# First layer norms of batches 4 to 7 one iteration later, keys of batch 1 ahead of the fourth row-max step

## What is computed

```python
x = x + _L0_xattn_ref(_layernorm(x), ctx_1024, ctx_1024, ...)   # 16 heads of 16, softmax over 375 keys
x = x + _L0_ffn_ref(_layernorm(x), ...)                         # 8 experts, top 1, capacity 112
x = x + _L1_xattn_ref(_layernorm(x), ctx_1024, ctx_1024, mask, ...)  # one head of 256
x = x + _L1_ffn_ref(_layernorm(x), ...)                         # 256 -> 1024 -> 256 with two low-rank terms
```

## Time and profile before

| | us |
|---|---|
| median of 3 executions | 358.65 |
| lowest, highest | 358.44, 359.33 |
| the profiled execution | 359.25 |
| span of the profiled execution | 357.5 |
| around the span | 1.75 |

### The profile page before, as it was taken

One profiled execution on the slowest core, in us unless ns is written; L12 is line 12 of the kernel. 1 busy time (PEld: TensorE's weight loads), 2 busy tenths in 40 slices (PEclk: granted clock), 3 DMA queues, 4 the chain that ended last, 5 costly groups with the idle time before them and its releaser, 6 DMA issues.

```text
span 357.5 us, 7953 instructions
## 1 busy us (share of the span) xinstructions
PE 343.3 (96%) x3128; PEld 261.9 (73%) x3128; DVE 189.3 (53%) x591; ACT 146.2 (41%) x340; POOL 57.7 (16%) x95
## 2 busy tenths in 40 slices
PE   7969999999999999998899999999899999999996
PEld 6535666676666666666689999888678789797875
DVE  4583656867766776855632212121889667441500
ACT  2416454565547454545442122112355675332400
POOL 3220400010101010101110000043774311200000
PEclk9989999999999999999999999999999999999999
DMA  8956051510001000044055899901110011101000
GB/s 223 331 184 219 18 203 36 184 67 2 16 2 44 2 13 4 16 162 149 15 144 208 264 311 336 307 30 51 52 28 3 17 42 53 53 29 52 28 26 26
DMA packets 24884, 35.28 MB, mean 99 GB/s; under 512 B 2608, under 2 KB 21408, under 8 KB 24736
## 3 DMA queue, kind: packets, MB, share of 16 engines
q1 hardware_dynamic: 22160, 31.73, 27.6%
q0 software_dynamic: 768, 1.84, 1.8%
q10 hardware_dynamic: 1920, 1.21, 1.3%
HBM read 31.06 MB, written 3.72 MB: 97 GB/s over the span
## 4 chain that ended last, share of the span: by engine, by line
PE 83%; DVE 5%; DMA 3%; issue 3%; ACT 3%; POOL 2%; ACTq 0%; DVEq 0%; POOLq 0%; SPq 0%
PE ps L659 8%; PE ps L804 8%; PE ps L669 8%; PE ps L782 7%; PE ps L495 6%; PE ps L422 6%; PE ps L515 5%; PE ps L450 5%; PE ps L536 4%; PE ps L558 4%; DMA w_in<-in_L_xattn_Wv 3%; PE ps L735 3%; PE ps L510 2%; PE ps L606 2%; PE ps L413 2%
## 5 line engine op out<-in xcount | busy, mean ns | idle before, releaser
L1141 DVE TENSOR_REDUCE mneg<-ps 112x2 f32<-112x750 f32 x64 | 56.9, 932 | 21.5 <-PE ps L495 21.5
L922 ACT ACTIVATE heads<-ps 125x896 f32<-125x896 f32 x34 | 29.3, 915 | 12.2 <-PE ps L515 12.2
L1370 POOL TENSOR_TENSOR rstd<-veps,neghalf 112x1 f32<-112x1 f32 x32 | 18.6, 581 | 95.9 <-DVE veps L1105 95.1
L495 PE MATMUL ps<-heads 32*112 32x375 f32 x256 | 30.5, 518 | 2.6 <-DVE mneg L1141 2.5
L659 PEld LDWEIGHTS ps<-xT,ring 128*128 128x128 f32 x256 | 29.8, 192 | 1.1 <-ACT xT L875 0.7
L659 PE MATMUL ps<-xT,ring 128*128 128x112 f32 x256 | 29.9, 275 | 0.4 <-ACT xT L875 0.4
L804 PE MATMUL ps<-heads,ring 128*112 128x256 f32 x128 | 28.8, 382 | 0.0
L669 PE MATMUL ps<-ring,heads 128*112 128x256 f32 x128 | 28.8, 379 | 0.0
L804 PEld LDWEIGHTS ps<-heads,ring 128*112 128x112 f32 x128 | 22.3, 177 | 6.1 <-issue 1.4
L450 PE MATMUL ps<-w_in,ctxT 128*125 128x256 f32 x96 | 26.5, 402 | 0.2 <-DMA w_in<-in_L_xattn_Wv 0.2
L515 PE MATMUL ps<-heads 32*125 32x224 f32 x384 | 25.6, 355 | 0.0
(11 more groups left out here) (150 smaller groups left out, 552.7 us busy)
## 6 DMA issues: line engine op xcount, KB each, us to landing
ring<-in_L_ffn_W SPq DMA_DIRECT2D x16, 1024.0 KB, 6.4
ctxT<-in_ctxT SPq DMA_DIRECT2D x8, 375.0 KB, 12.2
heads<-in_L_ffn_W SPq DMA_DIRECT2D x2, 1024.0 KB, 9.0
ring<-x_by_odd_rows_dram SPq DMA_DIRECT2D x4, 448.0 KB, 3.6
ring<-in_mask SPq DMA_DIRECT2D x1, 1312.5 KB, 6.9
expert_in_dram<-eo SPq DMA_DIRECT2D x1, 896.0 KB, 10.4
b2row<-in_L_ffn_b SPq DMA_DIRECT2D x8, 112.0 KB, 7.4
out_dram<-ring SPq DMA_DIRECT2D x8, 112.0 KB, 1.9
```

What stands on the lines that cost most here:

```text
L495: mm = pe.matmul(tile(("MX", b, g), j)[0:S, 0:S2], qz[rows, m, a, b * S:(b + 1) * S], kt[b % 3][rows, m, :], start=True, stop=True)
L922: act.activation(weights(b, step)[0:KC, js.start:js.stop, :], o[0:KC, :, 0:2 * QW], ACT.Exp, scale=DK ** -0.5).then_inc(free, 1)
L1141: v.tensor_reduce(mneg[:, b % 2, PAIRS * g + js.start:PAIRS * g + js.stop], o[0:S, :, 0:S2], AX.X, ALU.max, negate=True).then_inc(free, 1)
L1370: g.tensor_tensor(rstd[:, b:b + 1], veps[:, b:b + 1], neghalf[:, b:b + 1], ALU.pow)\
```

## The change

`EARLY` adds stages to slots, `MOVED` takes the same stages out of their old slots, and the entry of `FIRST_NORMS` for batches 4 and 5 goes from the front's slot 4 to iteration 0, that for batches 6 and 7 from iteration 0 to iteration 1. In the front NM0 of batch 0 goes from slot 4 to slot 5 behind the third row-max step, K1 of batch 1 goes from slot 6 to slot 5, ahead of that NM0 and of the fourth row-max step, and QX 1 goes from slot 4 to the end of slot 6. In iteration 0, NM1 of batch 0 goes behind V0 of batch 1.

```diff
+EARLY = {(-1, 5): [("K1", 1), ("NM0", 0)], (-1, 6): [("QX", 1)], (0, 0): [("NM1", 0)]}
+MOVED = {(-1, 4): [("NM0", 0)], (-1, 6): [("K1", 1)], (0, 0): [("NM1", 0)]}
...
-FIRST_NORMS = {(-1, 0): (2, 3), (-1, 4): (4, 5), (0, 4): (6, 7)}
+FIRST_NORMS = {(-1, 0): (2, 3), (0, 4): (4, 5), (1, 4): (6, 7)}
...
     for stage, behind in PIPE[u]:
         first = FIRST_K if stage[0] == "K" else 0
-        if first <= i - behind < NB:
+        if first <= i - behind < NB and (stage, i - behind) not in MOVED.get((i, u), ()):
             yield stage, i - behind
+    yield from EARLY.get((i, u), ())
     if (i % 2, u) in Q_SLOTS and (i + 3) // 2 < QCHUNKS and (i, u) != (-1, 2):
         yield Q_SLOTS[i % 2, u], (i + 3) // 2
-    if (i, u) == (-1, 4):
-        yield "QX", 1
```

## The result

| | before | after |
|---|---|---|
| median, us | 358.78 (4 executions) | 355.11 (4 executions) |
| lowest to highest | 358.44 to 359.33 | 354.55 to 356.19 |
| the profiled execution | 359.25, span 357.5 | 354.55, span 352.8 |

The account below looks back on a forecast made before the run. TensorE, busy 343.3 of 357.5 us, was taken as the bound. The front's -4.54 and +0.95 in iteration 1 gave -3.59: from the profiled 359.25 to 355.66, less 0.60 for the median, forecast 355.1 us, range 353.9 to 357.0.

Parts of the forecast that it names:

- The losses of the front: Front before the change: 5.26 us lost, as 0.47 ahead of NM0, 3.17 in the fourth row-max step, 1.62 by the clock.
- The new wait at the first scores: Front, first scores: their second strip waits for the bank pair of the fourth row-max step's first strip, 0.50 us.
- The new wait at K0 of batch 2: End of the front: K0 of batch 2 waits for ScalarE's copy of V0, which frees its spare bank, 0.22 us.
- The start: Front: TensorE ends V1 and V2 at 18.53 us (16.54 + 1.99), as before; the front's losses are counted from there.
- The moved norms: Iteration 1, fourth row-max step: norms of batches 6 and 7 make the second strip late, cost 0.95 us; iteration 0 unchanged.
- The sum: Whole kernel: front gain -4.54 plus 0.95 in iteration 1 gives -3.59 us.
- No cost for DMA: Front: context of batches 1 and 2 and first expert's weights, wanted or issued some 5 us earlier, cost nothing.
- Norms that block in iteration 1 as in the front: Rival, iteration 1: norms cost 3.17 and 1.62 by the clock; 358.9, no change; chance 0.05 with other ways.
- hide wholly: Rival, iteration 1: the moved norms cost TensorE nothing; 354.1 us, chance 0.05.
- The clock in the front: Rival, front: the granted clock falls there all the same, giving back 1.62 us; 356.7, chance 0.09.
- the 2.49 did it: Front before the change: only TensorE's idle 2.49 us was followed by a clock fall, waits of about half a microsecond weren't.

Follow-up runs that it names:

- e2_norms_only: The kernel before with only the change's FIRST_NORMS entries, stages standing as before; 356.53 us, ratio 0.9942.
- e4_hole_filled: The kernel before with eight extra matmuls on a spare bank between the two strips of the front's fourth row-max step; 358.50 us.
- e1_stages_only: The changed kernel's stage order with the first norms placed as in the kernel before; 361.04 us, ratio 1.0064 to the kernel before.
- e7_stages_filled: e1_stages_only with five extra matmuls on a spare bank between the strips of the front's fourth row-max step; 357.97 us.
- look3: One of four single profiled executions of the changed kernel, unedited; 356.51 us.
- e5_norms_apart: The changed kernel with the norms of batches 4 to 7 each alone, in slots where VectorE stands idle; 354.02 us, ratio 0.9865 to the kernel before.
- after_again: The changed kernel run again, unedited, with a further profile; 356.08 us over 12 executions.
- e6_values_ahead: e5_norms_apart with V0 of batch 1 ahead of the first scores and V1 behind them; 352.98 us, ratio 0.9833 to the kernel before.

## Why the prediction was right

The forecast of 355.1 with a range of 353.9 to 357.0 met 355.11, and by the median of all executions 355.6. The steps of the front and of iteration 1 came as forecast, each within 0.1 us. That the median was met to 0.01 us is luck: three of the first four executions had a clock of 1.00, of the next twelve only three, and those have 356.08, inside the range, with five executions (358.37 and more) outside it. Point by point, in the order of its sum:

- **The losses of the front** (0.47, 3.17, 1.62 by the clock). Confirmed: the 0.47 is still there in e2_norms_only (18.01) and gone in the changed kernel, with the norms gone the 3.17 shrink to about a third (1.1 us in e2_norms_only), and filling the hole returns 1.61 (e4_hole_filled), so the clock's fall in the front followed TensorE's standing still.
- **The new wait at the first scores, 0.50.** Measured: the second strip starts 21.66 - 21.09 = 0.57 us behind the first, and the scores take 1.69 (21.09 to 22.78) instead of 1.13, so 0.56.
- **The new wait at K0 of batch 2, 0.22.** Measured 24.99 - 23.94 - 0.83 = 0.22.
- **The start.** I took 18.53 as the end of the values, start plus duration; start to start it is 1.92, not 1.99. A duration in a timeline row includes the tail of the last matmul, which the next stage overlaps. The same slip of 0.07 is in both kernels and cancels in the sum.
- **The moved norms, 0.95.** Measured 0.92, and 3.07 us from the start of the norms to the reduces where 3.08 was taken from iteration 0.
- **The sum**, -3.59, against -3.56 between the traces when both are taken from the start of V1 and V2. Had I predicted the profiled execution, 355.66, it would have been off by 1.1 us, by what happened ahead of the change, the waits for weights among it; I hadn't seen that single executions differ by this much there.
- **No cost for DMA.** Right: nothing waits for the context or for the first expert's weights.
- **The rivals.** Norms that block in iteration 1 as in the front, or hide wholly: neither. The clock in the front: in no profile of the changed kernel, but not excluded for a quarter of its executions, and in e1_stages_only 1.3 us of idle time were enough. I had argued that short waits do nothing, since waits of half a microsecond did nothing, and that only "the 2.49 did it"; 1.30 did it too, and the price I gave the rival, 1.62, can be too low by a third or a half: in e1_stages_only against e7_stages_filled it was 2.4 us by the traces and 3.1 by the medians.
- **What no rival named.** The low clock at 245 us. Of the kernel before, 8 of 23 executions have a mean clock of 0.99 instead of 0.995 and a median of 360.0 instead of 358.3; in the traces the fall at 245 us costs 0.85 us from the last one-column matmuls to the second transpose of the next layer (244.01 to 251.99 in look3, 242.88 to 250.01 in the changed kernel's first profile). My range covered it by luck: it was made for other things.

## What to carry to other kernels

- A wait for one half of a resource can cost more than it shows: here a second strip that starts alone takes the whole 0.83 us again, because it would have run beside the first one (four matmuls alone take 0.89 us, eight 0.90). Take the loss from start to start of the stages, not from the idle time in brackets.
- Work that blocks an in-order engine is better placed where its consumer has long work of its own between two demands (here the weighted sums, 0.92 instead of 3.17 us), and better still split over slots in which the engine stands idle (e5_norms_apart, 354.02 us). Of two edits made together the one that looks like tidying (the order of the stages) may be worthless or harmful without the other: build each alone before crediting it.
- Before comparing two profiled executions, find the first stage where they part although the programs are the same; here 1.1 of 4.7 us arose ahead of the change, 0.6 of it in waits for weights.

## What the runs showed of the hardware

- The granted clock fell to half behind 2.49 us of idle TensorE for about 3.4 us, and behind 1.30 us of idle (between two single strips of row-max matmuls, 0.9 us each) for 6.8 us; it didn't behind 0.41 us (e2_norms_only), 0.51 us (e4_hole_filled) or 0.26 us (the changed kernel). The longer stop was not the dearer one. Two stops nearly as long as the 1.30 left the clock at full: 1.13 us of waiting for weights in e7_stages_filled (first row; the clock is 1.00 up to 20 us), and 1.23 us in the changed kernel near the end of the first attention (second row, and its window). Whether the length of a stop alone decides, or also what TensorE does around it, no run here separates.

```profile
10.52 1.78 PE L444 MATMUL ps<-xT,w_in 128*128 128x224 f32 x8 [1.13 <-DMA w_in<-in_L_xattn_Wq]
```

```profile
163.06 0.41 PE L415 MATMUL ps<-ident,xn 112*128 112x112 f32 x2 [1.23 <-DVE xn L1111]
```

```profile
162.00:163.00 1.00, 0.00 (x0) 0.00 (x0) 0.93 (x5) 0.43 (x1) 0.66 (x1) 1.00 0.04 13
```

- It also fell, in some executions and not in others of the same kernel, behind 2.1 us of one-column matmuls in which the profile has TensorE fully busy (look3, after_again, e1_stages_only, e2_norms_only, e6_values_ahead).
- The Trainium skill's warning (TensorE: Matmul & The Clock Gate, section "A second HAM failure mode: psum-queue depth-cycling") that short bank waits let the clock swing speaks of frequent ones. In e1_stages_only a single wait for a bank pair, 1.30 us, was followed by the low clock; for short waits, the changed kernel's among them, no trace here shows it.
- The second normalising instruction of a pair takes 0.80 us instead of 0.41 when GpSimd's addition starts just ahead of it. The Trainium skill has a rule for this (SBUF — State Buffer, section "Who interferes with whom": the two share a port pair, and the later one is blocked until the first is done). The rows fit it: in e5_norms_apart, where an addition starts 0.06 to 0.07 us ahead of each, each takes 0.80 to 0.82, and the first (28.56 to 29.36) ends 0.14 us behind its addition (28.49, 0.73 us each). They show the delay and not the port.
